# A decoder's last cross-attention: each batch's output product cut in two, and its sum taken one slot later

## The reference, cut to what matters

```python
q = lat @ Wq + bq                                  # lat: layernorm of the stream, (4, 512, 128)
kv = concatenate([context, lat], axis=1) @ Wkv + bkv   # context: 77 rows of each batch
k, v = split(kv, 2, axis=-1)
sim = einsum('bhid,bhjd->bhij', q * scale, k)      # 16 heads
attn = softmax(sim)
out = einsum('bhij,bhjd->bhid', attn, v)           # joined over heads: (4, 512, 1024)
x = layernorm(x + out @ Wout + bout)               # the output product: 1024 -> 128
```

## Time and profile before

| | us |
|---|---|
| three runs, in order | 1107.16, 1119.02, 1110.58 |
| median of the runs | 1110.58 |
| the profiled execution | 1109.02 |
| its span, first to last instruction | 1107.3 |
| mean granted TensorE clock over the span | 0.943 of full |

### The profile page before, as it was taken

The page is one execution under the profiler, slowest core; times in us unless marked ns, Lnnn a source line. Parts: engine busy times, 40 slices in busy tenths (PEclk is TensorE's granted clock), DMA queues, the critical chain, the costliest instruction groups (busy, mean ns, idle before and its releaser), DMA issues.

```text
span 1107.3 us, 16269 instructions
## 1 busy us (share of the span) xinstructions
PE 1011.8 (91%) x5218; PEld 799.3 (72%) x5218; DVE 725.4 (66%) x1589; ACT 704.1 (64%) x1397; POOL 569.4 (51%) x436
## 2 busy tenths in 40 slices
PE   6969989999999658899989999999999999998895
PEld 3747879888888536787768778878788887886432
DVE  5876665755655556787776777775867657761257
ACT  4336444343323444797976888886888868988453
POOL 7110230007365333677775777775777757777001
PEclk9979677999999858999999999999999999999998
DMA  7100000000000113131321323231313221310001
GB/s 237 7 1 1 1 1 2 1 1 1 1 1 1 38 41 83 41 82 43 78 47 42 75 50 82 51 75 42 80 45 84 56 66 44 83 42 1 1 1 38
DMA packets 46399, 46.14 MB, mean 42 GB/s; under 512 B 23095, under 2 KB 29163, under 8 KB 45803
## 3 DMA queue, kind: packets, MB, share of 16 engines
q1 hardware_dynamic: 46315, 45.10, 17.1%
HBM read 7.60 MB, written 1.05 MB: 8 GB/s over the span
## 4 chain that ended last, share of the span: by engine, by line
PE 80%; DVE 8%; ACT 4%; issue 4%; POOL 1%; DMA 1%; SPq 0%; POOLq 0%; DVEq 0%; ACTq 0%
PE PS L1581 77%; PE PS L1593 3%; DVE X_ODD L1096 1%; DVE BIG L1179 1%; DVE mx L1176 1%; DVE mxm L1442 1%; DVE st L1078 1%; ACT PHI L1028 1%; DVE X_EVEN L1096 1%; ACT BIG L1027 0%; POOL rs L639 0%; DVE mv L1084 0%; ACT BIG L784 0%; ACT BIG L776 0%; DMA QB<-TQ 0%
## 5 line engine op out<-in xcount | busy, mean ns | idle before, releaser
L734 POOL TENSOR_TENSOR PLO<-BIG,PHI 128x512 fp32r<-128x512 f32 (+1 forms) x320 | 414.1, 1294 | 184.1 <-ACT PHI L1028 172.7
L1027 ACT ACTIVATE BIG<-PS 128x512 f32<-128x512 f32 (+1 forms) x320 | 192.4, 601 | 98.7 <-PE PS L1581 93.2
L1442 DVE TENSOR_REDUCE mxm<-PS 128x1 f32<-128x512 f32 x256 | 174.2, 687 | 63.2 <-PE PS L1581 59.9
L1028 ACT ACTIVATE PHI<-PS 128x512 fp32r<-128x512 f32 (+1 forms) x320 | 191.2, 598 | 0.0
L639 POOL TENSOR_TENSOR rs<-ve,half_neg 128x4 f32<-128x4 f32 (+1 forms) x29 | 30.3, 1047 | 228.7 <-DVE ve L1086 227.9
L1581 PE MATMUL PS<-KA,QA 128*128 128x512 f32 (+1 forms) x512 | 138.9, 337 | 7.9 <-issue 7.6
L1581 PE MATMUL PS<-QA,KA 128*128 128x512 f32 (+1 forms) x320 | 129.7, 405 | 5.9 <-issue 5.6
L1581 PE MATMUL PS<-PHI,VLO 128*128 128x512 f32 (+1 forms) x320 | 131.2, 410 | 0.0
L1581 PE MATMUL PS<-PLO,VHI 128*128 128x512 f32 (+1 forms) x320 | 126.6, 396 | 1.0 <-POOL PLO L734 1.0
L1581 PE MATMUL PS<-QB,KB 128*128 128x512 f32 (+1 forms) x320 | 126.1, 394 | 0.0
L1581 PE MATMUL PS<-PHI,VHI 128*128 128x512 f32 (+1 forms) x320 | 126.0, 394 | 0.0
(11 more groups left out here) (263 smaller groups left out, 2012.2 us busy)
## 6 DMA issues: line engine op xcount, KB each, us to landing
KA<-TK SPq DMA_DIRECT2D x128, 128.0 KB, 2.3
QA<-TQ SPq DMA_DIRECT2D x64, 128.0 KB, 2.3
QB<-TQ SPq DMA_DIRECT2D x64, 128.0 KB, 2.3
KA<-TK SPq DMA_DIRECT2D x128, 19.5 KB, 1.8
X_EVEN<-in_x SPq DMA_DIRECT2D x4, 256.0 KB, 3.6
VXA<-in_L_ffn_Wg SPq DMA_DIRECT2D x1, 1024.0 KB, 5.7
VXA<-in_L_ffn_Wu SPq DMA_DIRECT2D x1, 1024.0 KB, 7.6
VXA<-in_L_ffn_Wd SPq DMA_DIRECT2D x1, 1024.0 KB, 9.2
```

The costliest lines, as they stand in the source:

```text
L734: pool.tensor_tensor(PLO[0:rows, g % 4, :], PX[0:rows, g % 4, :], PHI[0:rows, g % 4, :].bitcast(F32), ALU.subtract).then_inc(rest_pool, 1)
L1027: act.activation(PX[0:rows, g % 4, :], PS[0:rows, g % 2, :], ACT.Exp, scale=SCALE_W)
L1028: act.activation(PHI[0:rows, g % 4, :], PS[0:rows, g % 2, :], ACT.Exp, scale=SCALE_W).then_inc(lead_ready, 1)
L1442: dve.tensor_reduce(mxm[:, p % 2, h, m:m + 1], PS[:, 2 + g % 2, :], AX.X, ALU.max).then_inc(mu_free, 1)
```

## The change

The output product of batches 0, 1 and 2 is cut at two of its four tiles. The first half (`part` 0) still stands in slot 8 of the next batch's first pair, but behind that slot's value block V2 and no longer ahead of it; the second half (`part` 1) stands at the end of slot 9. The two share one place in the numbering of tasks and one bank, and only the second half signals `pj_full`. VectorE takes the sum into Y two slots after slot 8, in slot 0 of the next pair, in place of slot 9. The output product after the loop is as it was.

```diff
--- before.py
+++ after.py
@@ -185,6 +185,7 @@
 
 
 LAG = 3
+OUT_PARTS = {0: (0, 1), 1: (2, 3), None: range(NT)}
 HEAD_SLOTS = {5: 1, 9: 0}
 MAX_UNITS = {slot: (slot + 3) % SLOTS for slot in range(SLOTS)}
 REST_ON_VECTOR = ()
@@ -228,8 +229,6 @@
     if p + 1 < PAIRS:
         t[7] = [("c", p + 1)]
     b, hp = divmod(p, NHP)
-    if b and hp == 0:
-        t[8] = [("yE", b - 1)]
     for slot in range(8, SLOTS):
         if (p, slot) in OD_STEPS:
             t.setdefault(slot, []).append(("oD",) + OD_STEPS[p, slot])
@@ -239,6 +238,8 @@
     if ahead < B * QUARTERS:
         for j, slot in ((0, 5), (1, 7), (2, 8)) if p % 2 == 0 else ((3, 5), (4, 7)):
             t.setdefault(slot, []).append(("V", ahead, j))
+    if b and hp == 0:
+        t.setdefault(8, []).append(("yE", b - 1))
     return t
 
 
@@ -247,7 +248,7 @@
     return step_tasks(p - (slot == 0)).get((slot - 1) % SLOTS, []) if p or slot else []
 
 
-VECTOR_DELAY = {"Q": 2, "K": 2, "Kt": 2}
+VECTOR_DELAY = {"Q": 2, "K": 2, "Kt": 2, "yE": 2}
 
 
 def for_vector(p, slot):
@@ -1910,7 +1911,7 @@
                         ins = mm(PS[:, 2 + g % 2, w * t:w * t + w], QA[r][h][:, P * t:P * t + P], KA[r][h][:, S:KEYS_PAD])
                     ins.then_inc(mu_full, 1)
 
-            def task(key):
+            def task(key, part=None):
                 n = PJ[key]
                 if n >= 2:
                     pe.wait_ge(pj_free, n - 1)
@@ -1953,12 +1954,13 @@
                     pe.transpose(bank[0:2 * NT, 0:P], mxm[:, p % 2].rearrange("p h t -> p (h t)"), ident[:])
                     ins = pe.transpose(bank[0:2 * NT, P:2 * P], mxt[:, p % 2].rearrange("p h t -> p (h t)"), ident[:])
                 else:
-                    b = key[1]
+                    b, tiles = key[1], OUT_PARTS[part]
                     pe.wait_ge(on_ready, 2 * NHP * (b + 1))
-                    for t in range(NT):
+                    for t in tiles:
                         for c in range(NHP):
                             ins = mm(bank[:, P * t:P * t + P], OT[:, c, P * t:P * t + P], wout1s[:, c, :], start=c == 0, stop=c == NHP - 1)
-                ins.then_inc(pj_full, 1)
+                if part in (None, 1):
+                    ins.then_inc(pj_full, 1)
 
             for key in PROLOGUE:
                 if key[0] == "max":
@@ -1978,7 +1980,12 @@
                     if SLOTS * p + slot >= LAG:
                         pv(SLOTS * p + slot - LAG)
                     for key in tasks.get(slot, []):
-                        task(key)
+                        if key[0] == "yE":
+                            task(key, 0)
+                        else:
+                            task(key)
+                    if slot == SLOTS - 1 and p and p % NHP == 0:
+                        task(("yE", p // NHP - 1), 1)
             for late in range(LAG):
                 pv(SLOTS * STEPS - LAG + late)
 
```

## The result

| | before | changed |
|---|---|---|
| median of 20 runs, us | 1115.28 | 1117.46 |
| lowest and highest, us | 1096.15 to 1121.48 | 1109.48 to 1124.29 |
| mean of the 20 runs, us | 1113.1 +- 1.5 | 1117.3 +- 0.9 |
| ratio of the compared runs, 95% interval | | 1.0099 (1.0061 to 1.0136) |
| the profiled execution, us | 1109.02 | 1114.64 |

The ratio compares only runs within 1.5% of the fastest of their kernel, and with two runs of before at 1096 and 1099 that leaves 8 of its 20 (mean 1106.3) against all 20 of the changed kernel (mean 1117.3); the medians of all 20 lie 2.18 us, or 0.2%, apart, and their means 4.1 +- 1.8 us, or 0.37% (+- is one standard error throughout). So the measured ratio says about 11 us, the means of all runs say 4, the medians say 2, and the forecast said 2.2. Most of the 11 us comes from which runs are compared. The traces have to decide what the change did.

A forecast was written before the change was run, and what follows sets the result against it. TensorE was taken to bound the kernel; 0.2 us around pairs 8 and 9, 0.78 + 0.19 in pair 16 and 0.80 + 0.19 in pair 24 made 2.2 us, giving 1112.8 us, range 1106.5 to 1117.5.

The forecast's parts named there:

- What bounds the kernel: TensorE, busy 91% of the span; other engines idle behind the output product without stalling it, so splitting gains nothing directly.
- The wait for the bank: Behind V2, the output product waits until VectorE frees V1's bank: 0.57 us in pair 8, 0.78 in 16, 0.80 in 24.
- The switches: TensorE steps from fp32 products to scores twice, 0.14 us each, less 0.09: +0.19 us per boundary.
- The sum on VectorE: Moved to slot 0 of the next pair, it ends 3.08 us after the scores; 2.0 us to spare, no cost.
- What pair 9 absorbs: Pair 9's own 0.97 us stall takes up most of pair 8's 0.76 us delay, leaving 0.2 us.
- nothing is absorbed: Rival: pair 9's stall stays and pair 8 pays 0.76 us; 2.7 us in all, 1113.3 us; chance 0.18.
- The sum: Adding the costs around pairs 8, 16 and 24 gives 2.2 us, 1112.8 us against the median, or +0.2%.
- the halves feed the other engines: Rival: ScalarE and VectorE catch up, pair 9's stall vanishes, V1's rest is in time; -1.0 us, 1109.6 us; chance 0.1.
- nothing that a timing shows: For the whole kernel, the 2.2 us stay below the 1% (11 us) a measurement can tell; within 1%: 0.97.
- The clock rival: TensorE's clock falls to 1.2 GHz for one output product behind each new stall; +21 us, 1131.9 us; chance 0.01.
- Late sum: Rival: VectorE's late sum holds up K in slot 2 of pairs 9, 17, 25; 10.0 us, 1120.6 us; chance 0.03.
- does not do what it says: Rival: the split is not in the program; instruction order showed two runs of 16 products; no size or chance given.

The follow-up runs named there:

- order_only: The unchanged kernel with the output product whole in slot 8 but behind V2; loop 581.04 us against 578.23 before, ratio 1.0013.
- v1_early: The changed kernel with V1 made in slot 6 instead of 7 in a batch's first pair; loop 577.32 us, ratio 0.9992.
- late_sum: The changed kernel with the sum into Y taken one slot later, in slot 1 of the next pair; loop 580.45 us, one run.

## Why the prediction was right about the change and wrong about the time

**What bounds the kernel.** Right. The idle time of the other engines was cut in two and TensorE gained nothing. One reading was off, and nothing rests on it: the piece of 21.91 us begins with the product and ends in slot 7 of pair 9, so it holds less than one pair's work behind the product, and not two pairs' around it.

**The wait for the bank.** Right, and at its place: forecast 0.57, 0.78 and 0.80 us, measured 0.47, 0.80 and 0.80, each time behind V1's VLO. In pair 8 V2 takes longer from its start when it has itself waited: 600.82 to 601.16 for its first two products, where 0.23 was usual. order_only shows that the order makes the wait without any split; v1_early shows that it goes with the order of `c` and V1, while the halves stay.

**The switches.** Mis-sized, by little. The term had +0.19 us a boundary. Measured: the first half is 3.60 - 3.53 = 0.07 longer than half a product, the next two score products stand 0.31 apart instead of 0.23 behind the first half and 0.32 behind the second, and the second half is 3.48, 0.05 shorter. That is 0.07 + 0.08 - 0.05 + 0.09 - 0.09 = +0.10. Whole boundaries agree with that: 0.80 + 0.10 = 0.90, and pairs 23 to 25 grew by 42.53 - 41.61 = 0.92 on average, against 0.99 forecast.

**The sum on VectorE.** Right: it ended 2.85 us after slot 0's scores (forecast 3.08), and late_sum showed that a slot more is still free.

**What pair 9 absorbs.** This step of the sum failed, by little, and another error hid it. The term had TensorE 0.7 us late at pair 9 and 0.5 of it absorbed there. Measured, pair 8 costs 0.49 us (the table of the narrower stretch), and pair 9's stall was 0.88 us on average in the five traces of the unchanged kernel (0.59 to 1.20) and 0.84 in those of the changed one (0.45 to 1.21): 0.04 less, with a standard error of 0.2, so no absorption is shown. Pairs 7 to 9 grew from a mean of 44.79 to 45.24, by 0.45 +- 0.2 us. That lies between the term's 0.2 and the 0.76 of the rival "nothing is absorbed", whose mechanism fits at least as well as mine and whose price was too high. The forecast 0.2 was too low by some 0.25, and the switches too high by 0.09 at each of two boundaries, so the total came out right in part by luck.

The first half of the step did happen. Slot 3's exponential in pair 9 came 0.66 us after the scores in all five traces, where it had been 1.15, and TK was written 7.50 us after slot 0's scores where it had been 7.87. But the landing doesn't follow TK. SyncE's queue in the changed kernel, which answers to its row:

```profile
618.52 0.46 SPq L572 DMA_DIRECT2D KA<-TK  x1
619.02 1.57 SPq L573 DMA_DIRECT2D KA<-TK  x1
620.64 0.71 SPq L572 DMA_DIRECT2D KA<-TK  x1
621.39 0.60 SPq L573 DMA_DIRECT2D KA<-TK  x1
```

And before:

```profile
615.39 0.46 SPq L571 DMA_DIRECT2D KA<-TK  x1
615.89 0.60 SPq L572 DMA_DIRECT2D KA<-TK  x1
616.53 1.41 SPq L571 DMA_DIRECT2D KA<-TK  x1
```

The first issue is 0.42 us earlier than before (8.22 us after slot 0's scores, 8.64 before). Then one of the issues takes 1.57 us here and 1.41 before, and the fourth, which the prediction had named, comes 11.14 us after slot 0's scores on average of five, against 11.16 before. What holds the queue in the long issue is not shown.

**The sum.** Forecast 2.2 us. The loops of the five traces of each kernel have means of 578.23 and 580.49: 2.26 us, with single traces up to 0.7 off their mean. The rival "the halves feed the other engines" was wrong in its time, though ScalarE did catch up. The medians of the first comparison, 2.18 us apart, agree by luck: by the scatter of the runs they could as well have been -1 or 8.

**The step that failed** is the one from the sum to what a measurement shows: "nothing that a timing shows", with a median that "can stand some 3 us below or 4 above this one by its own scatter". The measured ratio was 1.0099, its interval leaves out 1, and the moved work explains 0.002 of it. All runs against all give 0.0037 here, and 4.2 +- 1.0 us over all sets; the rest of the 0.0099 comes from comparing 8 of the 20 runs of before with all 20 of the changed kernel. I had taken the scatter from three runs and hung the range on their median, 1110.58, as if it were the kernel's. The median of before was 1115.28 in the next comparison, and its mean between 1109.4 and 1113.0 in four later ones; its 170 runs reach from 1095.3 to 1125.0, so 30 us where the three had shown 11.9. The scatter comes for the most part from stages ahead of the loop. The page of before had shown them, in its row of the granted clock by 40 slices (tenths of full speed, 9 for 90% or more), where the loop lies in the row of nines from slice 17 on:

```profile
PEclk9979677999999858999999999999999999999998
```

Seven of the first 16 slices stand at 5 to 8, and I had looked at the clock only in the loop, where it is 1.00. What is shown is that a kernel whose loop is as long as before's gives the same ratio (1.0101 and 1.0136), and that the changed kernel is 1.4 us slower at equal clock. Why its mean clock is 0.0030 lower, three standard errors, is open: by chance, or by something that a changed program does to the stages ahead of the loop.

**The clock rival** was wrong for the loop. Its place was the new stalls, and in no trace did the loop leave 1.00 there.

**Late sum, and "does not do what it says":** wrong, as forecast.

## What to carry to other kernels

Other engines' idle time behind a long product is no gain to be had unless the busy engine waits afterwards: look at the rows behind it first. When a step in a ring of two buffers is moved, count anew which step it now stands two behind, and when that one's reader is done; that took 0.8 us here, and in the traces making that step one slot earlier gave more back (3.3 us) than the change had cost (2.3). Where the expected effect is a few us of 1100, compare a stretch between two rows that both programs have: it was good to 0.7 us in one trace here, when the timed runs of each kernel differed by 1% in the wrong place. And where a ratio is formed from the fastest runs of each side, look at how many each side keeps: 8 of 20 against 20 of 20 turned 0.4% into 1.0% here.

## What I had not expected of the hardware

The stages ahead of the loop, the same instructions in every kernel here, took between 428 and 453 us, by the clock that TensorE was granted there (0.68 to 0.86 in the windows shown), with TensorE busy for 94 to 95% of each window shown. In the loop, at a clock of 1.00, stretches of over 100 us without the boundaries (pairs 9 to 15, 17 to 23) agreed to 0.12 us over all traces.
